# Other rows for the stacked q and k of a decoder block's attention, and one max tile at an earlier place

## The reference

```python
nx = _ln(x, ln1_scale, ln1_bias)
q, k, v = split_heads(nx @ W_qkv)
x = x + attend(q, k, v, causal) @ W_self_out
nx = _ln(x, ln2_scale, ln2_bias)
q = heads(nx @ W_q);  k, v = heads(encoder_output @ W_kv)      # 154 keys
x = x + attend(q, k, v, None) @ W_cross_out
nx = _ln(x, ln3_scale, ln3_bias)
return x + relu(nx @ W1 + b1) @ W2 + b2
```

## Time and profile before

| | |
|---|---|
| median of 3 runs | 1010.27 us (1007.81 to 1012.84) |
| the profiled execution | 1010.27 us, its span 1008.5 us |
| TensorE busy | 970.3 us, 96% |
| VectorE, ScalarE, GpSimd busy | 751.5, 644.2, 250.8 us |
| DMA queue of SP | 122.73 MB, 37.1% of 16 engines' span |

### The profile page before, as it was taken

How to read it: one execution, slowest core, us unless ns; L and a number is a source line. 1 busy time by engine, 2 the same in 40 slices (tenths; PEclk the granted TensorE clock), 3 DMA queues, 4 the chain that set the end, 5 groups by cost and what they waited for, 6 DMA issues and landing times.

```text
span 1008.5 us, 20064 instructions
## 1 busy us (share of the span) xinstructions
PE 970.3 (96%) x7632; PEld 611.2 (61%) x7632; DVE 751.5 (75%) x1173; ACT 644.2 (64%) x1380; POOL 250.8 (25%) x444
## 2 busy tenths in 40 slices
PE   3899999999999999999999998999999999999998
PEld 2786665555555555555544664444444599999997
DVE  6778778999999999999942787688887644555542
ACT  4553337777777777777788334688887744445443
POOL 6422122232222222232244210011112222222210
PEclk9998999999999999999999998799999999999999
DMA  6696573131313232323414896234441111221001
GB/s 199 232 354 239 189 245 118 58 103 55 103 60 109 66 109 66 109 66 109 169 48 135 275 365 233 71 109 151 143 137 48 42 63 64 63 64 47 29 31 42
DMA packets 78272, 124.01 MB, mean 123 GB/s; under 512 B 10624, under 2 KB 51872, under 8 KB 73120
## 3 DMA queue, kind: packets, MB, share of 16 engines
q1 hardware_dynamic: 78176, 122.73, 37.1%
HBM read 72.48 MB, written 49.17 MB: 121 GB/s over the span
## 4 chain that ended last, share of the span: by engine, by line
PE 87%; DVE 9%; ACT 1%; issue 1%; DMA 1%; SPq 0%; POOL 0%; ACTq 0%; DVEq 0%
PE bank L847 20%; PE bank L828 18%; PE bank L706 11%; PE bank L687 10%; PE bank L688 9%; PE bank L689 9%; DVE mx L1203 6%; PE bank L882 3%; PE bank L679 3%; PE bank L714 2%; PE bank L674 2%; DVE nx_mem L1189 1%; PE bank L727 1%; ACT probs L1090 1%; DVE probs L1196 1%
## 5 line engine op out<-in xcount | busy, mean ns | idle before, releaser
L1090 ACT ACTIVATE probs<-bank 128x512 f32<-128x512 f32 (+3 forms) x1024 | 455.2, 526 | 123.6 <-PE bank L828 118.5
L1203 DVE TENSOR_REDUCE mx<-bank 128x2 f32<-128x1024 f32 (+5 forms) x416 | 433.9, 1083 | 43.2 <-PE bank L706 28.5
L828 PE MATMUL bank<-q_st,k_st 64*128 64x512 f32 (+3 forms) x1024 | 288.9, 431 | 5.7 <-ACT probs L1090 3.2
L828 PEld LDWEIGHTS bank<-q_st,k_st 64*128 64x128 f32 x1024 | 136.0, 186 | 180.7 <-ACT probs L1090 164.1
L847 PE MATMUL bank<-probs,nx_mem 128*32 128x512 f32 (+3 forms) x2048 | 232.0, 530 | 2.6 <-ACT probs L1090 1.3
L706 PE MATMUL bank<-k_st,q_st 62*128 62x154 f32 (+4 forms) x1280 | 228.1, 351 | 6.0 <-DVE mx L1203 4.0
L706 PEld LDWEIGHTS bank<-k_st,q_st 62*128 62x128 f32 x1280 | 145.5, 189 | 50.5 <-DVE mx L1203 33.3
L1554 POOL TENSOR_SCALAR_AFFINE_SELECT probs<-probs 128x256 f32<-128x256 f32 x256 | 103.8, 407 | 205.6 <-ACT probs L1090 205.1
L1563 POOL TENSOR_TENSOR oN<-oT,rs 128x256 f32<-128x256 f32 x64 | 41.6, 650 | 219.6 <-DVE rs L1298 219.5
L1137 ACT ACTIVATE hT<-bank,b_sb 128x512 f32<-128x512 f32 x64 | 44.2, 690 | 70.3 <-PE bank L689 70.3
L1446 DVE TENSOR_TENSOR hT_lo<-hT,hT_hi 128x512 fp32r<-128x512 f32 x64 | 42.7, 687 | 57.3 <-ACT hT_hi L1140 56.3
(11 more groups left out here) (122 smaller groups left out, 1280.1 us busy)
## 6 DMA issues: line engine op xcount, KB each, us to landing
q_st<-q_parts SPq DMA_DIRECT2D x48, 256.0 KB
q_st<-qx_parts SPq DMA_DIRECT2D x48, 256.0 KB
xt<-in_x_dram SPq DMA_DIRECT2D x16, 512.0 KB, 5.9
q_parts<-probs SPq DMA_DIRECT2D x16, 512.0 KB, 4.3
k_parts<-probs SPq DMA_DIRECT2D x16, 512.0 KB, 3.6
k_st<-k_parts SPq DMA_DIRECT2D x32, 256.0 KB
qx_parts<-probs SPq DMA_DIRECT2D x16, 512.0 KB, 6.7
v_aug<-vst_mem SPq DMA_DIRECT2D x8, 544.0 KB, 5.3
```

Source lines behind the costliest of these rows:

```text
L828: pe.matmul(bank[:, score_bank(a, use), 0:n], keys_of(a, v0)[rows, i // 2, P * kb:P * kb + P], q_st[w][rows, i // 2, lo:lo + n], start=Tru ...
L1090: act.activation(probs[:, use % NPT, 0:n], bank[:, score_bank(a, use), 0:n], ACT.Exp, scale=SCALE).then_inc(a.exp_done, 1)
L1203: dve.tensor_reduce(mx[:, par, part].rearrange("p (j y) -> p j y", j=2)[:, :, blocks.start:blocks[-1] + 1:blocks.step], banks[:, :, 0:len( ...
```

## The change

The rows of a stack are laid out in runs. In each half of 64 partitions, row 2 * d + s holds part s (0 and 1) of row d, and row 32 + d the third part. q's first two parts are the same, and its run reads one part twice. So each side has four transfers, two for each half, of 32 and of 16 neighbouring partitions. Rows 48 to 61 are the spare ones. In `EARLY_X` one place goes, (5, 0), and one comes, (3, 1). The count that a unit's first max tile waits for is written anew.

```diff
-    PARTS = {"q": (0, 0, 1), "k": (0, 1, 0)}
-    TRANSFERS = {"q": 4, "k": 5}
+    RUNS = {"q": ((0, 0, 2, True), (2, 1, 1, False)), "k": ((0, 0, 2, False), (2, 0, 1, False))}
...
-        EARLY_X = {4: (1, 3), 5: (0, 1, 3), 6: (0, 2, 3), 7: (0, 1, 2, 3)}
+        EARLY_X = {3: (1,), 4: (1, 3), 5: (1, 3), 6: (0, 2, 3), 7: (0, 1, 2, 3)}
...
-                    for r, part in enumerate(PARTS[side]) if side in sides else ():
-
-                        rows = src[u, part].rearrange("(g r i) t -> g r i t", g=2, i=2)[w % 2]
-                        if r < 2 or side == "q":
-                            sp.dma_start(st[w][r:P:4, :, :].bitcast(F32), rows).then_inc(a.stack_in[w], 16)
-                        else:
-
-                            for j in range(2):
-                                sp.dma_start(st[w][HALF * j + r:HALF * j + HALF - 4:4, :, :].bitcast(F32),
-                                             rows[DK * j:DK * j + DK - 1]).then_inc(a.stack_in[w], 16)
-                        if r == 2:
-                            sp.dma_start(st[w][3:P:HALF, :, :].bitcast(F32), rows[DK - 1:2 * DK:DK]).then_inc(a.stack_in[w], 16)
+                    for j in range(2):
+                        for r, first, count, repeated in RUNS[side] if side in sides else ():
+                            rows = one(src, u).rearrange("u s (g j d a) t -> d (u s) g j (a t)", g=2, j=2, d=DK)[:, :, w % 2, j]
+                            rows = (rows[:, first:first + 1].to_broadcast([DK, count, 2 * L]) if repeated
+                                    else rows[:, first:first + count])
+                            p0 = HALF * j + DK * r
+                            sp.dma_start(st[w][p0:p0 + DK * count, :, :].bitcast(F32),
+                                         rows.rearrange("d s (i t) -> d s i t", i=2)).then_inc(a.stack_in[w], 16)
...
-                    n_q, n_k = TRANSFERS["q"], TRANSFERS["k"]
-                    pe.wait_ge(a.stack_in[w], 16 * (n_q * (v0 // 4 + 1) + n_k * (v0 // 4 + 1 if a.causal else 1)))
+                    pe.wait_ge(a.stack_in[w], 16 * 8 * (v0 // 4 + 1) if a.causal else 16 * 4 * (v0 // 4 + 2))
```

## The result

The changed kernel took 1022.91 us (median of 4 runs, 1021.60 to 1026.06) against 1010.63 us before: a ratio of 1.0128, 95% interval 1.0093 to 1.0163. It is slower by 12.3 us, where the prediction had 6.2 and its range ended at 1022.0. The profiled execution has a span of 1020.2 us.

A forecast was written before the change was run, and what follows sets the result against it. TensorE, busy 96% of the span with no slack and no DMA wait to remove, was taken as the bound. A 3.7 us wait plus 2.5 us of clock made 6.2 us on 1010.3: 1016.5 us, range 1009.0 to 1022.0.

The forecast's parts named there:

- The wait at the moved tile: Dense stage, pass 3, place (3, 1): TensorE asks for the q stack at 584.1, it lands at 587.8; 3.7 us.
- the working: The prediction's estimate of the cross q stack's landing: last issue done at 583.33, landing at 587.8.
- the rate in part 5: Rate of the new cross q load behind the moved tile's wait: 2.1 to 4.8 us for 0.79 MB, taken as 2.1.
- the first row: 377 GB/s, reached by a lone cross q load at 671; gave 2.1 us for the new load.
- the other row: 164 GB/s, the lowest half microsecond with self attention's stacks in flight; gave 4.8 us for the new load.
- the self tile: Self attention's first max tile, using its stack at 64.99: no wait in the sum, 1.8 us in the narrow writes rival.
- the rival of narrow writes: Transfers into 32 or 16 neighbouring partitions are slow; waits at cross and self tiles, late maxima: 1021.0 to 1022.0 us, chance 0.23.
- The clock: TensorE's clock falls to half after the pause in pass 3: 1.7 to 3.3 us, taken as 2.5.
- the fall at 84 to 91: Clock at 0.53 in the kernel before, soon after a 1.8 us wait; used to price a fall at 3.3 us.
- the entry: Entry to cross attention, 17 us at half clock; a rival had its 8.3 us gone or short, 1005.7 us, chance 0.10.
- The sum: Pass 3 wait of 3.7 us plus clock fall of 2.5: 6.2 us, +0.6%, 1016.5 us; chance 0.33.
- The parts at nothing: Matmuls unchanged, fewer issues covered (0.5 us per self attention unit), count of 8 free, tile's 0.5 us moved: all worth 0.

The follow-up runs named there:

- the third profile: The unmodified changed kernel, profiled a third time to see whether the wait at self attention's first max tile varies by execution: 1016.85 us, span 1015.1.
- the halves: Two kernels, each with one part of the change against the kernel before: new stack rows with the tile left, 1012.02 us; old rows with the tile moved, 1013.35 us.
- the place alone: The kernel before with its old stack rows and only the max tile moved from (5, 0) to (3, 1): 1013.35 us, ratio 1.0031.
- the new rows alone: The changed kernel's stack rows with the max tile left at (5, 0), against the kernel before: 1012.02 us, ratio 1.0016.

## Why the prediction was wrong

- **The wait at the moved tile: right.** That it appears, once, at (3, 1), ahead of the projection of pass 3, and that nothing gives it back is in every profile with the new place, but for the two in which matmuls of no use fill it. With the old rows it was 3.0 us, the stack landing 3.8 us after its last issue against 4.5 in the working.
- **The step that failed is the rate in part 5.** It read "I take 2.1, since the queue at 584 is full and near the first row, and keep 4.8 for the range". The new load took an estimated 3.8 us, and the wait was 5.3 us (4.8 to 6.6 over four profiles) instead of 3.7. The shape of the destinations sets the engines' time, with a full queue as with an empty one: 145 and 190 GB/s with the engines at 1.01 and 0.98, where the old rows have 352 and 384. The row that I held nearest was of the old shape. Nor did the other row show a slow shape: at 175.5 the 164 GB/s go with engines busy 0.57 of the time, so that its 4.8 us lie on the right side is luck.
- **Put at nothing with it: the self tile.** The sum had nothing for it, since TensorE waited for no stack in that stage; the rival of narrow writes had 1.8 us. It was 3.4, 2.5, 1.9 and once 0 us.
- **The clock: right in kind, short in size.** I took 2.5 us for one fall. Behind the cross tile 9 us at 0.62 cost 3.4 us, behind the self tile 16 us at 0.57 cost 6.9 us, and a fall at 550, with no wait ahead of it, cost 1.7. On the other side the fall at 84 to 91 went away (3.3 us), and the entry lost 3.4 us instead of 8.5. In all 17.3 - 14.1 = 3.2 us more in this profile. The entry's gain didn't last: the other three profiles lost 8.4 to 8.6 us there, and the clock took 6.4, 1.1 and 13.7 us more than before.
- **The sum again:** 9.0 us of waits and 3.2 of clock are 12.2 us; the span grew by 11.7. The rival of narrow writes named the mechanism, both places and the late maxima rows, and came to 1021.0 to 1022.0, close to the 1022.91. That closeness is in part luck: it had 6.4 us at the cross tile for 5.3, 1.8 at the self tile for 3.4, and 2.5 of clock for 3.2.
- **The predicted number does occur, by luck:** the third profile, without the self wait, took 1016.85 us against 1016.5. But its cross wait was 5.4 us for 3.7, and the clock took 1.1 us for 2.5. Of the 13 runs of the changed kernel one more, at 1016.31, lies there.
- **The parts at nothing held** as far as the rests show it: fewer issues, same matmuls, the tile's own 0.5 us. In self attention TensorE is as busy as before, though the DMA engines are not.

Why the halves have ratios of 1.0016 and 1.0031 and the whole 1.0128: the place alone makes a cross wait of 3.0 us, and only the narrow load makes it 5.3 and more, with a longer fall behind it (3.4 us instead of 1.7). The self wait needs the narrow rows alone, and whether it comes is the execution's. Part of the difference between these medians is that chance, and how the chances stand for each kernel was not measured: a self wait of 1.9 us or more came in three of four profiles of the changed kernel and in none of four of the new rows alone.

## What to carry to other kernels

Before the rows of a DMA's destination are rearranged, lay the partitions of the old and of the new transfer side by side: a shorter list of transfers with the same bytes took 1.4 times (32 rows) and 2 times (16 rows) the engines' time here. Slack on a load is only proven where the load is asked for; a use that moves earlier has to be set against the landing of the neighbours in the queue. A wait of TensorE in a dense stage is to be priced with what follows it: waits of 3.0, 5.3 and 3.4 us had 1.7, 3.4 and 6.9 us at half clock behind them. And an added matmul fills a pause only if it stands ahead of it: look for it in the trace before its time is read.

## What the runs showed of the hardware

- Transfers of 8 KB rows from DRAM: 313 GB/s of busy engines into every fourth of 128 partitions, 219 into 32 neighbours, 138 into 16 neighbours, and about 275 for 16 rows spread over 64 or 128. In a full queue, with other transfers beside them: 352 and 384 GB/s with the old rows, 145 and 190 with the new.
- Little transfers queued behind narrow loads (the maxima rows) took a median of 4.2 us to land over the whole kernel, where they took 1.9 with the old rows.
- A stack whose transfers go to the two halves of the partitions by turns landed 12.1 us after its first issue, where in the other order, with a full queue, it took 13.6 to 15.1. The cross stack had no such gain (9.3 against 9.1 to 9.7).
- The changed kernel lost 15 to 28 us to the clock from one profiled execution to the next, the new rows alone 12 to 20.
